# A decoder layer on one Trainium2 core: line-aligned rectified values, a reordered VectorE program in the expert stage, and the seventh block sum on GpSimd

## The reference

```
scores = x @ Wr + br                       # 8 experts
mask = the two highest scores, others 0
router_output = softmax(mask)
h = relu(einsum('btd,edh->bteh', x, W1) + b1)      # hidden 1024
expert_outputs = einsum('bteh,ehd->bted', h, W2) + b2
x = layernorm(x + einsum('bte,bted->btd', router_output, expert_outputs))
```

## Time and profile before

| What | Value |
|---|---|
| median of 3 runs | 1704.68 us (1700.19 to 1710.17) |
| the profiled execution, its own time | 1695.43 us |
| its span, first to last instruction | 1693.3 us |
| outside the span | 2.1 us |
| expert stage | 973.7 us to the end of the span |
| TensorE busy | 1609.9 us, 95% |
| VectorE busy | 1247.9 us, 74% |
| GpSimd busy | 1088.8 us, 64% |
| ScalarE busy | 1053.2 us, 62% |

### The profile page before, as it was taken

The page is one execution under the profiler, slowest core; times in us unless marked ns, Lnnn a source line. Parts: engine busy times, 40 slices in busy tenths (PEclk is TensorE's granted clock), DMA queues, the critical chain, the costliest instruction groups (busy, mean ns, idle before and its releaser), DMA issues.

```text
span 1693.3 us, 31002 instructions
## 1 busy us (share of the span) xinstructions
PE 1609.9 (95%) x9777; PEld 1243.9 (73%) x9777; DVE 1247.9 (74%) x3965; ACT 1053.2 (62%) x3137; POOL 1088.8 (64%) x1520
## 2 busy tenths in 40 slices
PE   6899999999999999999998899999999999999995
PEld 5586786776777867767767478877777777777774
DVE  4668767877787678777776576578787878787866
ACT  1566847948758579478486644555555555555552
POOL 2566756847757567467475655758585858585853
PEclk9899999999999999999999899999999999999998
DMA  7203003012021030120211011101010110101001
GB/s 220 66 2 83 20 22 81 2 45 57 3 71 31 13 89 2 44 59 2 61 36 52 1 51 39 63 13 51 25 44 32 37 39 28 47 20 56 13 1 50
DMA packets 54946, 70.77 MB, mean 42 GB/s; under 512 B 12736, under 2 KB 41024, under 8 KB 54784
## 3 DMA queue, kind: packets, MB, share of 16 engines
q1 hardware_dynamic: 54064, 66.04, 13.8%
q10 hardware_dynamic: 720, 2.75, 0.5%
HBM read 37.23 MB, written 2.16 MB: 23 GB/s over the span
## 4 chain that ended last, share of the span: by engine, by line
PE 75%; DVE 8%; POOL 6%; ACT 6%; issue 5%; DMA 0%; DVEq 0%; POOLq 0%; ACTq 0%
PE ps_Y L2409 21%; PE ps_S L1452 17%; PE ps_H L2409 17%; PE ps_O L1452 5%; PE ps_X L1452 5%; PE ps_T L1681 5%; ACT pr L892 4%; POOL pr L728 3%; PE ps_T L1452 2%; PE ps_T L1801 1%; POOL rot L668 1%; PE ps_S L1801 1%; DVE sm L1363 1%; DVE h_sb L2325 1%; POOL rot L678 1%
## 5 line engine op out<-in xcount | busy, mean ns | idle before, releaser
L2089 POOL TENSOR_TENSOR h_lo<-h_sb,h_hi 128x512 fp32r<-128x512 f32 x256 | 376.0, 1492 | 186.4 <-ACT h_sb L2125 185.7
L693 POOL TENSOR_TENSOR pr<-pr,rden 128x128 f32<-128x128 f32 (+2 forms) x768 | 308.0, 438 | 83.6 <-DVE rden L1244 83.3
L892 ACT ACTIVATE pr<-sm,nmx 128x128 f32<-128x128 f32 (+2 forms) x768 | 311.6, 413 | 22.2 <-DVE nmx L1255 22.2
L2124 ACT ACTIVATE h_hi<-h_sb,b_sb 128x512 fp32r<-128x512 f32 x224 | 161.0, 719 | 169.8 <-DVE h_sb L2325 169.8
L728 POOL TENSOR_TENSOR pr<-pr,rden 128x256 f32<-128x256 f32 x256 | 150.9, 616 | 110.9 <-DVE rden L1244 110.8
L1255 DVE CUSTOM_DVE_ANT_0 sm<-ps_S,cmask 128x128 f32<-128x128 f32 (+2 forms) x768 | 192.6, 308 | 33.0 <-PE ps_S L1452 24.0
L2409 PE MATMUL ps_Y<-h_hi,w_hi 128*128 128x512 f32 x512 | 203.8, 398 | 5.9 <-POOL h_lo L2089 5.9
L2325 DVE TENSOR_TENSOR h_sb<-ps_H,part 128x512 f32<-128x512 f32 x168 | 116.0, 691 | 125.9 <-PE ps_H L2409 120.9
L2409 PE MATMUL ps_Y<-h_lo,w_hi 128*128 128x512 f32 x512 | 203.1, 397 | 0.0
L2409 PE MATMUL ps_Y<-h_hi,w_lo 128*128 128x512 f32 x512 | 202.9, 396 | 0.0
L946 ACT ACTIVATE pr<-sm,nmx 128x256 f32<-128x256 f32 x256 | 127.9, 502 | 50.6 <-DVE nmx L1363 50.4
(11 more groups left out here) (308 smaller groups left out, 3737.0 us busy)
## 6 DMA issues: line engine op xcount, KB each, us to landing
qT_sb<-rot SPq DMA_DIRECT2D x256, 64.0 KB, 2.0
w_raw<-in_W SPq DMA_DIRECT2D x16, 1024.0 KB, 6.5
kT_sb<-rot SPq DMA_DIRECT2D x192, 64.0 KB, 2.0
share<-shares SPq DMA_DIRECT2D x16, 512.0 KB, 3.6
xin<-in_x SPq DMA_DIRECT2D x8, 256.0 KB, 2.8
cin<-in_ctx SPq DMA_DIRECT2D x8, 256.0 KB, 2.6
w_kw<-in_wink ACTq DMA_DIRECT2D x2, 768.0 KB, 6.0
w_ks<-in_selk SPq DMA_DIRECT2D x2, 768.0 KB, 5.7
```

What stands on the lines that cost most here:

```text
L693: last = pool.tensor_tensor(p_, p_, rden[:, h % 2, n:n + 1].to_broadcast([P, width]), ALU.mult)
L892: last = act.activation(pr[:, h % PR_SLOTS, a:a + width], sm[:, h % 2, a:a + width], ACT.Exp, bias=nmx[:, h % 2, n:n + 1], scale=-1.0, acc ...
L2089: pool.tensor_tensor(h_lo[:, g % RING, k, :], h_sb[:, k, :], h_hi[:, g % RING, k, :].bitcast(F32), ALU.subtract).then_inc(low_sb, 1)
L2124: act.activation(h_hi[:, g % RING, k, :], src, ACT.Relu, bias=bias)
```

## The change

Six edits in `expert_stage`:

1. `half_line` goes, and `h_hi` and `h_lo` are made with the helper, so that both start on a 64-byte line.
2. The seventh sum, c22 + p5, moves from VectorE to GpSimd. It stands between the second and third `h_lo` of its block, waits for the sixth sum, and ScalarE's rectification of tile 3 waits for it (`pool_sum`).
3. `last_rows` comes first in VectorE's program, `route` second, and all 36 operations of `differences` follow.
4. `high_slice` precedes `outputs` in blocks in which both stand.
5. At the end TensorE computes the outputs of block 62 alone, and then those of block 63.
6. VectorE's end: the additions to `total` follow their readings one by one, and the last four tiles' variances stand behind the last addition.

```
-        sb("half_line", [P, 8])
-        h_hi = ctx.enter_context(nc.sbuf_tensor("h_hi", [P, RING, 4, CH], F32R))
-        h_lo = ctx.enter_context(nc.sbuf_tensor("h_lo", [P, RING, 4, CH], F32R))
+        h_hi = sb("h_hi", [P, RING, 4, CH], F32R)
+        h_lo = sb("h_lo", [P, RING, 4, CH], F32R)
...
         # gpsimd, block g, tile k
+                    if k == 2 and g >= DENSE:
+                        pool.wait_ge(sum_out, sums_of(g, 6))
+                        pool.tensor_tensor(h_sb[:, 3, :], h_sb[:, 3, :], part[:, 1, :], ALU.add).then_inc(pool_sum, 1)
...
         # scalar
-                    act.wait_ge(sum_out, sums_of(g, (1, 5, 6, 7)[k]))
+                    if k < 3:
+                        act.wait_ge(sum_out, sums_of(g, (1, 5, 6)[k]))
+                    else:
+                        act.wait_ge(pool_sum, g - DENSE + 1)
...
         # vector
-                sum_(c22, c22, p5)
...
                 if g == 0:
+                    last_rows()
+                if g == 1:
+                    route()
+                if g == 2:
                     dve.wait_ge(*ends.rows_done)
                     differences(0, 0)
-                if g == 1:
-                    last_rows()
                     differences(0, 1)
-                if g == 2:
-                    route()
...
-                if q == 0 and g:
-                    outputs(g // NQ - 1)
                 if g % DENSE == NQ + 1 and e + 1 < NE:
                     mixed_weights(e + 1)
                 if slice_after(g):
                     high_slice(*slice_after(g))
+                if q == 0 and g:
+                    outputs(g // NQ - 1)
...
+            dve.wait_ge(y_read, 4 * last + 3)
+            dve.tensor_tensor(total[:, 0, NTOK - CH:NTOK], ...scaled[:, 0, :], ALU.add).then_inc(total_done, 1)
             for group in (4, 5):
                 add_turned(group)
+            output(last, 3).then_inc(y_read, 1)
+            dve.wait_ge(y_read, 4 * last + 4)
+            dve.tensor_tensor(total[:, 1, NTOK - CH:NTOK], ...scaled[:, 1, :], ALU.add).then_inc(total_done, 1)
             for t in range(TILES2, TILES2 + TT):
                 dve.wait_ge(turn_read, t + 1)
                 variances([t])
-            output(last, 3).then_inc(y_read, 1)
-            ... the two additions
...
         # tensor
-            last = [QUADS - 2, QUADS - 1]
+            last = [QUADS - 1]
+            outputs([QUADS - 2])
             outputs(last, range(3))
```

More of the change, by code:

```diff
@@ L1976, in expert_stage @@
         full = [sem(f"hidden_full_{b}") for b in "abcd"]
-        part_out, sum_out = sem("part_out"), sem("sum_out")
+        part_out, sum_out, pool_sum = sem("part_out"), sem("sum_out"), sem("pool_sum")
         rect_sb, low_sb = sem("rectified_sb"), sem("rectified_low")
@@ L1993, in sums_of @@
         def sums_of(g, n):
-            return 7 * (g - DENSE) + n
+            return 6 * (g - DENSE) + n
         def tiles_of(g, n):
@@ L1999, in y_bank @@
         def y_bank(g, b):
-            return 4 * min(g, QUADS - 2) + b + 1
+            return 4 * g + b + 1
         def slice_after(g):
@@ L2384, in _ @@
             output(last, 2).then_inc(y_read, 1)
+            dve.wait_ge(y_read, 4 * last + 3)
+            dve.tensor_tensor(total[:, 0, NTOK - CH:NTOK], total[:, 0, NTOK - CH:NTOK], scaled[:, 0, :], ALU.add
+                              ).then_inc(total_done, 1)
             for group in (4, 5):
                 add_turned(group)
+            output(last, 3).then_inc(y_read, 1)
+            dve.wait_ge(y_read, 4 * last + 4)
+            dve.tensor_tensor(total[:, 1, NTOK - CH:NTOK], total[:, 1, NTOK - CH:NTOK], scaled[:, 1, :], ALU.add
+                              ).then_inc(total_done, 1)
             for t in range(TILES2, TILES2 + TT):
@@ L2567, in _ @@
                 outputs([g - 1], range(2))
-                pe.wait_ge(sum_out, sums_of(g, 7))
+                pe.wait_ge(sum_out, sums_of(g, 6))
                 pe.wait_ge(total_done, 4 * (STEPS - 1))
@@ L2573, in _ @@
             hidden(QUADS - 1)
-            last = [QUADS - 2, QUADS - 1]
+            last = [QUADS - 1]
+            outputs([QUADS - 2])
             outputs(last, range(3))
-            pe.wait_ge(sum_out, sums_of(QUADS - 1, 7))
+            pe.wait_ge(sum_out, sums_of(QUADS - 1, 6))
             pe.wait_ge(total_done, 4 * (STEPS - 1) + 2)
```

## The result

| | before | after |
|---|---|---|
| median of 4 runs | 1704.55 us (1700.19 to 1710.17) | 1735.17 us (1730.44 to 1741.37) |
| ratio, 95% interval | | 1.018 (1.0136 to 1.0224) |
| span of the profiled execution | 1693.3 us | 1733.3 us |
| expert stage in it (first hidden product to the end) | 719.7 us | 755.0 us |

The change makes the kernel 31 us slower. The profiled executions differ by 40.0 us, of which 4.7 lie in the attentions, where no instruction changed: TensorE's first hidden product starts at 973.68 us before and at 978.35 after. In the tables "stage" is that difference.

What follows compares the result with a forecast made beforehand. TensorE, busy 95%, bounds the kernel, so only its matmul pace and its waits count. Terms -7.6 + 37.8 + 0.7 + 9.4 - 4.0 = +36.3 us gave 1731.7 profiled, 1741.0 with 9.2 added for the median; range 1700 to 1758.

Steps and rivals of the forecast that it cites:

- alignment: Expert-stage output matmuls: aligned operands cover 32 lines instead of 33, 6.7 ns less per settled matmul, -7.6 us in 64 blocks.
- casts and seventh sum, in the blocks: GpSimd full, VectorE's casts and additions held up: 4.4 us plus 1.9 of clock in six blocks, +37.8; late bank copies, +0.7.
- hand-over: Start of expert stage: router wait gone, 5.3 us won; outputs(4) waits 12.8 us behind 18 moved differences, 14.7 lost: +9.4.
- end, with the later last `h_lo`: Last blocks: outputs(62) fill the 5.93 us wait, though the seventh sum delays the last `h_lo`: -4.0 us.
- rival B: Output matmuls: the alignment brings nothing, total +43.9 us, 1748.6 us; chance 0.15.
- The forward count: Blocks 16 to 17, VectorE operation by operation: first sum done at 1170.35, TensorE going on 4.4 us later than before.
- The time at the lower clock: Behind TensorE's long waits in blocks 17, 25, ... 57: matmuls at the lower clock level lose 1.9 us each time.
- That the two had to be costed together: Casts ahead of outputs and seventh sum on GpSimd, counted as one term with block 16 as the example: +37.8 us.
- Block 14: Block 14 and its likes: ScalarE's later rectification of tile 3 delays its bank copy, 0.1 us seven times, 0.7 us.
- A: Block 16 and its likes: casts fall into GpSimd's gap, old stalls go, -7.5 us in all, 1697.2 us; chance 0.22.
- C: Slice blocks: GpSimd's backlog carries over, ScalarE's bank copies 1 us late in three, seven experts: +21 us, 1762; chance 0.13.

Runs made afterwards that it cites:

- after_noalign: The changed kernel with only the alignment undone (`half_line` back as before): 1745.90 us, ratio 1.026 against the kernel before.
- casts_poolsum: The kernel before with `high_slice` ahead of `outputs` and the seventh sum on GpSimd, nothing else: 1737.81 us, ratio 1.022.
- handover: The kernel before with only VectorE's new order at the hand-over (`last_rows`, `route`, then `differences`): 1710.44 us, ratio 1.007.
- casts: The kernel before with only `high_slice` put ahead of `outputs` in blocks that have both: 1724.63 us, ratio 1.014.
- align: The kernel before with only `half_line` removed, so that `h_hi` and `h_lo` start on a 64-byte line: 1681.08 us, ratio 0.990.
- poolsum: The kernel before with only the seventh sum moved from VectorE to GpSimd: 1719.08 us, ratio 1.010.

## Why the prediction was right

Direction, size and range held: 1741.0 us forecast, 1735.17 measured (+36.3 and +30.6). Term by term, each against the difference of the expert stages. In the last column the alignment is the changed kernel against `after_noalign`, and the others are `after_noalign` against the kernel before, stretch by stretch:

| Term | forecast | alone | together |
|---|---|---|---|
| alignment | -7.6 | -16.3 | -10.1 |
| casts and seventh sum, in the blocks | +38.5 | +39.8 | +37.5 |
| hand-over | +9.4 | +9.6 | +9.3 |
| end, with the later last `h_lo` | -4.0 | -3.5 | -1.5 |
| sum | +36.3 | | +35.3 |

- **Alignment, the term that was mis-sized.** The step was to take the hidden products of the seven-product blocks as aligned, because they start on a 64-byte line, and to let only 15 of 24 output matmuls gain in full. In fact all 24 gain, and the 21 hidden matmuls of a block gain 5 ns each, most likely because `dif_hi` and `dif_lo` move with `half_line`. The 232 ns of "aligned" seven-product blocks, which I counted as evidence for rival B, were the trace's hint that 64 bytes is not the measure. The Trainium skill (TensorE: Matmul & The Clock Gate, "Wait — 56ns, not 53.3ns?") has no term for the address, and by it nothing would have changed. The measurement decides: 226.7 against 232 and 233.4 ns. The ends given, 0 and 10.3 us, did not hold the 16.3. They hold the 10.1 of the changed kernel by luck only, since that a faster TensorE gains less where it waits was not in the sum.
- **Casts and seventh sum.** The forward count put the end of block 17's first sum 9.43 us behind the start of hidden(17) (1170.35 against 1160.92). It is 9.45 (1181.75 against 1172.30). The block grows by 6.6 us in `casts_poolsum` (18.09 against 11.46), where I had 6.3. In the changed kernel blocks 17, 25, ... 57 last 17.9 us on the mean, 6.7 over 10.20 and the old 1.0. The time at the lower clock was a little short: I took 1.9 us for it from two other waits, and it is 1.7 in three of the six blocks and 2.7 to 2.9 in the others, 2.2 on the mean. VectorE's casts and additions and GpSimd's operations do alternate at 1.4 to 1.7 us, as the exclusive lock of the Trainium skill (SBUF — State Buffer, "SBUF: two separate sides") has it; the trace agrees.
- **That the two had to be costed together** was not needed. Each stalls the block alone, and they add up. My reason for the casts' stall, that GpSimd is full, holds only with the seventh sum; without it the early slices do it.
- **Block 14:** 0.1 us forecast, 0.3 measured (10.50 against 10.20). The mechanism, ScalarE's late bank copy, is there: six of the 13 waits in the row of weight loads below, 0.4 us each, lie in blocks 14, 22, ... 54. The others are in blocks 17, 25, ... 57, ahead of the long wait, and two of 0.2 us in blocks 28 and 33.
- **Hand-over.** A wait of 12.8 was forecast and 12.9 measured. The won 5.3 and the lost 14.7 are as counted: in `handover` hidden(0) to hidden(3) takes 31.35 us instead of 36.77, hidden(3) to hidden(6) 47.92 instead of 33.33.
- **End.** The last `h_lo` ends 13.6 us behind the start of hidden(63), and not 12.4, so TensorE waits 2.9 us instead of 2 and runs slowly behind. Additions to `x` start 21.7 us behind hidden(63), against 22.6 before and a forecast of 18.9. So little is left of the 4 us: without the alignment the last stretch is 1.5 us shorter than before, with it 1.4. From the single runs the term looks right (-3.5); together it was sized 2.5 us too large.
- **Rivals.** A came half true in `casts` and shows why it could not win. B is excluded by `align`. C's late bank copies cost a third of a microsecond in one block of eight, not 1 us in three.

The forecast is therefore right for its mechanisms. That it comes within 1 us of the stage's +35.3 is luck: in the changed kernel the alignment brings 2.5 us more than forecast and the end 2.5 less. And the alignment is that near only because a second omission, nothing for what is lost of it in waits, makes up for part of the first.

```profile
PEld ps_H L2415 <- ACT part L2138: 4.9, 13, 0.5
```

This is the row of the weight loads' waits on ScalarE's copies in the changed kernel.

## What to carry to other kernels

Moving work of an engine that is not the bottleneck to another that looks idle is to be counted forward from the block where both have the most to do: shares of 64% and 74% did not tell that one block of eight had no room. When a producer is put earlier, ask what its consumer then runs beside; here the released subtractions cost the additions more than the casts had cost. And a gap of some bytes ahead of one tensor moves every tensor behind it, or, where starts are rounded up, none at all, so compare the addresses of all moving operands in the two programs.

## What was not expected of the hardware

- Matmuls of 512 columns whose moving operands all start on a multiple of 128 bytes settled at 226.7 ns. With all operands 32 bytes behind one they went at 233.4, and with operands at 0 and 32 or at 0 and 64 alternating the whole run went at 232 to 233.
- With all operands 64 bytes behind, the same 24 matmuls went at 229 ns in 33 blocks and at 233.3 in 20 blocks of one execution.
- Behind a run at another pace, dense blocks of the kernel before needed nine matmuls until they settled. The 21 matmuls of its seven-product blocks, which alternate operands at 0 and 64, did not settle at all.
- A faster TensorE changed its own waits: with the alignment alone the waits of 0.8 us in blocks 13, 21, ... went, and those in blocks 17, 25, ... grew to 1.6.
- Waits of the same length were followed by stretches at the lower clock of very different length: in `poolsum`, behind 1.8 us of waiting, none in two blocks and 7 or 8 matmuls in four; in the changed kernel, behind waits of 5 us, 7 to 14 matmuls.
